# The first row group's adjacency of a graph attention kernel in eight transfers in place of sixteen

## The chip, the core and the metric

The kernel runs on one core of a Trainium2 chip. TensorE (PE) multiplies and transposes, VectorE (DVE), ScalarE (ACT) and GpSimd (POOL) do the rest, SyncE (SP) only issues transfers. Each engine works its own instructions in order and waits on semaphores. Transfers are issued by SP, ACT or POOL into a queue each and are carried out by 16 DMA engines that all queues share; a transfer is cut into packets, and its semaphore stands at 16 when all engines are done. The metric is the device time of one execution in microseconds (us): 810.08 us is the median of three runs (810.04 to 810.56).

## What is computed

One graph attention layer over 8192 nodes with 128 features, after a normalisation, with a residual:

```python
def _L0_gnn_ref(h, adj, W, a):
    Wh = h @ W                                   # 8192 x 128
    f1 = Wh @ a1 ; f2 = Wh @ a2                  # a score half for each node
    e = leaky_relu(f1[:, None] + f2[None, :], negative_slope=0.2)
    e = where(adj == 0, -inf, e)                 # adj: 8192 x 8192 int32, zeros and ones
    return softmax(e, axis=1) @ Wh
h = maximum(_layernorm(x, axis=-1), 0.0)
x = x + _L0_gnn_ref(h, adj, W, a)
```

The adjacency is 268 MB of int32. It is read once, and turned into bytes on the way, so that a value takes 4 bytes in DRAM and 1 byte in SBUF.

## The kernel before, in words

**Tiling.** The 8192 rows are 16 row groups of 512 (`NQ`); a partition holds four neighbouring rows of its group (`PACK`). The 8192 columns are 16 units of 512 (`UN`), four of which (`KC`) are a column group of 2048 (`CHUNK`). For each row group and each unit the kernel needs the adjacency of 512 by 512, transposes it, forms the weights and multiplies them into four accumulators.

**A unit's way.** ACT scales half of the unit's bytes (`second`, line 591), POOL adds the halves so that two edges share a byte (`mix`, line 239), PE transposes them (`transposes`, line 382), ACT unpacks the result into `marks` (`unpack`, line 571), DVE makes four tiles of weights (`weights`, line 811), and PE does 32 products with them (`product`, lines 392 and 396).

**The first row group** is worked while the features of all nodes are still being made, 4 tiles of nodes (a group `g` of 512 nodes) for each unit `b`. A loop of 16 steps `b` runs on all engines. In step `b` PE does the products of unit `b`, the features of group `b + 2` (line 365), and the transposes of the normalised x of group `b + 3` (line 349). ACT does `second(b + 3)`, keeps the features (`keep`, line 549), takes the exponentials (lines 561, 562), unpacks unit `b + 2`, applies the ReLU (line 542), and normalises a quarter of group `b + 4`. POOL does `mix(b + 2)`, `scaled(b + 2)` (line 267), three quarters of the normalisation of group `b + 4` (line 248), and issues transfers. DVE does the weights of unit `b + 1` with `low_part` (line 801), `pack(b + 2)` (lines 792, 793), and in the steps that the tables name the statistics of x (`statistics`, line 751) and the inverse roots of a batch (`inverses`, lines 768 to 773). All of this stands in an order written out by hand; in DVE's step 2 it is `first_weights(3)`, `inverses(3)`, `pack(4)`, `statistics(10)`, and in step 3 `first_weights(4)` comes next.

**Loading x.** x is 4 MB of float32 and comes in five batches of groups, `BATCHES = [(0, 1), (1, 4), (4, 6), (6, 10), (10, 16)]`, issued by SP (line 182). The first two are issued at once. Batches 2, 3 and 4 are held back by a wait on the adjacency of units 0, 1 and 3 (line 188). The first use of batch 3 is `statistics(6)` in DVE's step 0, the first use of batch 4 is `statistics(10)` in DVE's step 2.

**Loading the adjacency.** The first row group comes unit by unit: `load_part(u)` on POOL (line 224) moves, for 128 partitions and four rows of each, 512 values, 2 KB of DRAM into 512 bytes of SBUF, and has a semaphore of its own, `first_loaded[u]`. Units 0 to 9 are issued ahead of all other work of POOL (`EARLY`), units 10 and 11 ahead of the loop, 12 in step 0, 13 in step 1, 14 and 15 in step 2 (`PARTS`). All later row groups come in transfers of one row of a column group: 128 partitions of 2048 values each, 8 KB of DRAM into 2 KB of SBUF (`load`, line 214); the first of these are issued from step 3 on (`FIRSTS`, `HALVES`). POOL's and SP's transfers stand in two queues, q0 and q1 of the profile. POOL's is worked in the order of issue.

Of the kernel before, what the change touches and what calls it, by code (L numbers as in the profile page):

```python
# [38 lines left out]
P = 128  # L39
PACK = 4  # L40
BANK = 512
CHUNK = PACK * BANK
# [17 lines left out]
def gat_kernel(nc, x, adj, W, a, out):  # L60
# [5 lines left out]
    KC = CHUNK // BANK  # L66
    UN = NC * KC
# [3 lines left out]
    AHEAD = 6  # L71
    EARLY = 10
    HALF = PACK // 2
# [10 lines left out]
    MIXES = {13: (15, 16), 14: (17, 18), 15: (19,)}  # L84
    PARTS = {0: (12,), 1: (13,), 2: (14, 15)}
    FIRSTS = {3: 4, 6: 5, 10: 6, 14: 7}
# [6 lines left out]
    with ExitStack() as ctx:  # L93
# [6 lines left out]
        def sem(name):  # L100
# [4 lines left out]
        masks = sb("masks", [P, GC, CHUNK], U8)  # L105
# [31 lines left out]
            "adj_second0", "adj_second1", "adj_second2", "adj_second3",  # L137
            *(f"first_loaded{u}" for u in range(UN)),
            "ident_zero", "ident_ready", "cst_ready", "rows_done", "out_stored", "x_again",
# [8 lines left out]
        adj_second = [s[f"adj_second{c}"] for c in range(NC)]  # L148
        first_loaded = [s[f"first_loaded{k}"] for k in range(UN)]
        x_loaded = [s[f"x_loaded{k}"] for k in range(len(BATCHES))]  # L150
# [3 lines left out]
        adj_dram = adj.rearrange("(q p s) (c k) -> q s c p k", p=P, s=PACK, k=CHUNK)  # L154
        adj_first = adj.rearrange("(q p s) (b k) -> q b p s k", p=P, s=PACK, k=BANK)

# [55 lines left out]
        def _(pool):  # L212
# [8 lines left out]

            def load_part(u):
                c, k = u // KC, u % KC
                nc.gpsimd.dma_start(masks[:, c * PACK:(c + 1) * PACK, k * BANK:(k + 1) * BANK],  # L224
                                    adj_first[0, u]).then_inc(first_loaded[u], 16)

            for u in range(EARLY):
                load_part(u)
# [61 lines left out]
            mix(1)  # L290
            scaled(1)
            load_part(EARLY)
            load_part(EARLY + 1)
            for b in range(UN):
                for u in MIXES.get(b, (b + 2,)):
                    mix(u)
                if b + 2 < NQ:
                    scaled(b + 2)
                if b + 4 < NQ:
                    normalise(b + 4)  # L300
                for u in PARTS.get(b, ()):
                    load_part(u)
                if b in FIRSTS:
                    load_first(FIRSTS[b])
                if b in HALVES:
                    load_second(HALVES[b])
# [689 lines left out]
```

## Time and profile before

| | |
|---|---|
| median of three runs | 810.08 us (810.04 to 810.56) |
| profiled execution | 810.9 us, its span 809.2 us |
| PE busy | 785.9 us, 97% |
| DVE busy | 740.8 us, 92% |
| ACT busy | 483.5 us, 60% |
| POOL busy | 419.2 us, 52% |
| POOL's transfer queue (q0) | 67.13 MB written to SBUF, 87.8% of the DMA engines' time |
| DRAM read | 272.70 MB |

Times inside the span count from its start. The profiled execution took 1.7 us more than its span, and 0.8 us more than the median of the runs. Bytes and GB/s of a transfer are those that are written; a transfer of the adjacency reads four times as many. A packet is one run of values: four rows in each of 128 partitions make 512 packets for a unit, and 16 packets of 4 bytes raise the semaphore. The number of an issue that a landing belongs to is found by taking a narrow window of time around that issue.

### The profile page before, as it was taken

The page shows a single profiled execution, that of the slowest core. Times are in us where ns is not written, and L with a number is a line of the kernel's source. Part 1 is how long each engine was busy: PE and PEld are TensorE (multiplying, and loading weights), DVE is VectorE, ACT ScalarE, POOL GpSimd, SP SyncE. Part 2 cuts the span into 40 slices and gives each one's busy share as a digit, 9 for nine tenths or more (in the row PEclk, how much of TensorE's full clock was granted, in tenths as well). Part 3 has the DMA queues.
Part 4 walks back from the last instruction along what each step waited for, and adds up shares of the span by engine and source line. Part 5 has one row for each costly group of instructions (what it writes and reads, how often), then busy time and mean ns, then how long its engine had stood idle before and what let it go on. Part 6 is the DMA issues. An engine that isn't in the chain of part 4 may idle for free.

```text
span 809.2 us, 22590 instructions
## 1 busy us (share of the span) xinstructions
PE 785.9 (97%) x8969; PEld 718.5 (89%) x8969; DVE 740.8 (92%) x1189; ACT 483.5 (60%) x777; POOL 419.2 (52%) x621
## 2 busy tenths in 40 slices
PE   5899999999999999999999999999999999999997
PEld 4778799999999999999999999999999999999986
DVE  6997899999999999999999999999999999999996
ACT  6788865655655565565555556565555656555542
POOL 7687755544545554454545445454544545454320
PEclk9999999999999999999999999999999999999999
DMA  9998899999999999999999999999999999998200
GB/s 172 169 106 85 79 108 114 110 96 107 85 101 95 97 91 88 110 85 101 91 100 91 87 110 86 101 88 104 90 88 107 89 100 86 106 90 87 27 14 17
DMA packets 48321, 75.99 MB, mean 94 GB/s; under 512 B 4768, under 2 KB 13600, under 8 KB 48288
## 3 DMA queue, kind: packets, MB, share of 16 engines
q0 software_dynamic: 43008, 67.13, 87.8%
q1 hardware_dynamic: 4864, 8.39, 3.1%
q8 instruction: 17, 0.28, 0.1%
q14 instruction: 16, 0.13, 0.0%
q10 hardware_dynamic: 416, 0.07, 0.0%
HBM read 272.70 MB, written 4.19 MB: 342 GB/s over the span
## 4 chain that ended last, share of the span: by engine, by line
PE 90%; issue 3%; ACT 2%; DVE 2%; POOL 2%; DMA 1%; ACTq 0%; POOLq 0%; DVEq 0%
PE acc L392 53%; PE acc L396 27%; PE stage L382 7%; PE stage L365 2%; DVE wt_ring L811 1%; PE stage L373 1%; ACT ht L542 1%; DMA a_sb<-in_L_gnn_a_dram 1%; PE stage L349 1%; POOL xn L248 0%; ACT wh L549 0%; POOL tmp L267 0%; POOL masks L224 0%; POOL masks L239 0%; ACT tmp L562 0%
## 5 line engine op out<-in xcount | busy, mean ns | idle before, releaser
L811 DVE SCALAR_TENSOR_TENSOR wt_ring<-stage,packed,marks 128x512 f32<-128x512 f32 x1024 | 697.6, 743 | 54.1 <-PE acc L396 42.5
L392 PE MATMUL acc<-pairs,wt_ring 128*128 128x258 f16 x4096 | 718.9, 274 | 2.4 <-DVE pairs L801 1.3
L396 PE MATMUL acc<-pairs,wt_ring 128*128 128x129 f16 x4096 | 697.4, 219 | 0.0
L392 PEld LDWEIGHTS acc<-pairs,wt_ring 128*128 128x128 f16 x4096 | 396.0, 97 | 56.7 <-DVE pairs L801 2.2
L571 ACT ACTIVATE marks<-stage 128x1024 uint16<-128x1024 uint8 x256 | 262.0, 1023 | 290.5 <-PE stage L382 289.3
L396 PEld LDWEIGHTS acc<-pairs,wt_ring 128*128 128x128 f16 x4096 | 399.5, 98 | 2.5
L239 POOL TENSOR_TENSOR masks<-masks 128x256 int32<-128x256 int32 x256 | 184.2, 734 | 240.4 <-ACT masks L591 239.6
L214 POOL DMA_DIRECT2D masks<-in_adj_dram x240 | 130.3, 545 | 99.5 <-PE stage L382 77.5
L591 ACT ACTIVATE masks<-masks 128x512 uint16<-128x512 uint16 x256 | 158.9, 622 | 0.5 <-DMA masks<-in_adj_dram 0.5
L382 PE MATMUL stage<-ident,masks 128*128 128x128 f32 x512 | 99.2, 276 | 1.5 <-POOL masks L239 0.9
L382 PEld LDWEIGHTS stage<-ident,masks 128*128 128x128 f32 x512 | 53.0, 141 | 6.4 <-issue 2.8
L365 PE MATMUL stage<-wx,ht 128*128 128x130 f32 x124 | 22.2, 305 | 6.8 <-ACT ht L542 5.8
L365 PEld LDWEIGHTS stage<-wx,ht 128*128 128x128 f32 x124 | 17.7, 205 | 10.5 <-ACT ht L542 9.1
L267 POOL TENSOR_TENSOR tmp<-wh,tmp 128x512 f32<-128x512 f32 x16 | 17.9, 1120 | 16.5 <-ACT tmp L562 16.5
L274 POOL TENSOR_SCALAR fin<-fin 128x516 f32<-128x516 f32 x15 | 22.8, 1523 | 0.3
L608 ACT ACTIVATE fin<-acc 128x258 f32<-128x258 f32 x60 | 19.6, 388 | 3.2 <-PE acc L392 3.2
L248 POOL TENSOR_SCALAR xn<-xm,small 128x128 f32<-128x128 f32 x42 | 18.2, 441 | 1.9 <-DVE small L773 1.9
L614 ACT ACTIVATE fin<-fin,inv 128x128 f32<-128x128 f32 x60 | 19.0, 389 | 0.0
L549 ACT ACTIVATE wh<-stage 128x260 f32<-128x260 f32 x31 | 12.0, 387 | 10.8 <-PE stage L365 10.7
L284 POOL TENSOR_TENSOR xm<-fin,xm 128x512 f32<-128x512 f32 x15 | 18.0, 1203 | 0.1
L277 POOL TENSOR_TENSOR fin<-fin 128x516 f32<-128x516 f32 x15 | 16.5, 1102 | 1.3
L751 DVE BATCH_NORM_STATS2 stats<-xm 128x6 f32<-128x256 f32 x32 | 11.5, 415 | 3.1 <-DMA xm<-in_x_dram 3.1
(60 smaller groups left out, 143.9 us busy)
## 6 DMA issues: line engine op xcount, KB each, us to landing
masks<-in_adj_dram POOLq DMA_DIRECT2D x256, 256.0 KB, 7.4
out_dram<-xm SPq DMA_DIRECT2D x15, 256.0 KB, 7.2
xm<-in_x_dram SPq DMA_DIRECT2D x1, 1536.0 KB, 13.4
xm<-in_x_dram SPq DMA_DIRECT2D x1, 1024.0 KB, 10.5
xm<-in_x_dram SPq DMA_DIRECT2D x1, 768.0 KB, 5.8
xm<-in_x_dram SPq DMA_DIRECT2D x1, 512.0 KB, 7.6
xm<-in_x_dram SPq DMA_DIRECT2D x1, 256.0 KB, 3.2
out_dram<-xm SPq DMA_DIRECT2D x4, 64.0 KB, 2.6
```

What stands on the lines that cost most here:

```text
L214: nc.gpsimd.dma_start(masks[:, c * PACK + r, :], adj_dram[q, r, c]).then_inc(adj_loaded[c] if r < 2 else adj_second[c], 16)
L239: nc.gpsimd.tensor_tensor(edges4[:, c, 0, :, sl], edges4[:, c, 0, :, sl], edges4[:, c, 1, :, sl], ALU.add).then_inc(s["mixed"], 1)
L274: nc.gpsimd.tensor_scalar(fin[:, :, E1:2 * E1], fin[:, :, E1:2 * E1], 1.0 / LOW, None, ALU.mult).then_inc(s["lows_scaled"], 1)
L365: mm = nc.tensor.matmul(to[:, r * 256:r * 256 + WC], ht[:, g % 2, k:k + P], wx[:], start=(r == 0), stop=(r == 1), skip_group_check=True)
L382: mm = nc.tensor.transpose(stage[:, 0, r * P:(r + 1) * P], words[:, c * PACK + r, kk * P:(kk + 1) * P], ident[:])
L392: return nc.tensor.matmul(acc[:, r, 0:2 * E1], wtv[:, w, r, 1, :], pairv[:, t, :, 0:E1], start=st, stop=end)
L396: return nc.tensor.matmul(acc[:, r, 0:E1], wtv[:, w, r, 0, :], pairv[:, t, 0, 0:E1], start=False, stop=False)
L571: nc.scalar.activation(split[:, b % MR, :].rearrange("p (s w) -> p s w", s=PACK), stage[:, 0, 0:BANK // 2].bitcast(U8).rearrange("p (w s) ...
L591: nc.scalar.activation(twos[:, c, 1, :, sl], twos[:, c, 1, :, sl], ACT.Copy, scale=SECOND).then_inc(s["second_ready"], 1)
L608: nc.scalar.activation(fin[:, r, :], acc[:, r, 0:2 * E1], ACT.Copy).then_inc(s["acc_free"], 1)
L614: mm = nc.scalar.activation(fin[:, r, 0:Fo], fin[:, r, 0:Fo], ACT.Identity, scale=inv[:, r:r + 1])
L811: nc.vector.scalar_tensor_tensor(out=wtq[:, t % NW], in0=e_row, scalar=packed[:, t, 1:2], in1=edges[:, k], op0=ALU.max, op1=ALU.mult).then ...
```

## The change

The first row group's adjacency comes in eight transfers. `GROUPS` lists the units of each: four transfers of one unit, two of two units, two of four units, which is a whole column group. A transfer still has 128 partitions with four rows of each, so 512 packets whatever its width; a packet is now 2 KB, 4 KB or 8 KB of DRAM. Each transfer has one semaphore, and `first_loaded[u]` is the semaphore of the transfer that holds unit `u`. The first seven (units 0 to 11) are issued ahead of all other work of POOL, the eighth (units 12 to 15) ahead of the loop. The loop issues none of them, and the table `PARTS` is gone.

```diff
-    EARLY = 10
+    GROUPS = [(0, 1), (1, 2), (2, 3), (3, 4), (4, 6), (6, 8), (8, 12), (12, 16)]
+    EARLY = 7
...
-    PARTS = {0: (12,), 1: (13,), 2: (14, 15)}
...
-            *(f"first_loaded{u}" for u in range(UN)),
+            *(f"first_loaded{k}" for k in range(len(GROUPS))),
...
-        first_loaded = [s[f"first_loaded{k}"] for k in range(UN)]
+        first_loaded = [s[f"first_loaded{k}"] for k, (lo, hi) in enumerate(GROUPS) for u in range(lo, hi)]
...
-        adj_first = adj.rearrange("(q p s) (b k) -> q b p s k", p=P, s=PACK, k=BANK)
+        adj_first = adj.rearrange("(q p s) (c k) -> q c p s k", p=P, s=PACK, k=CHUNK)
...
-            def load_part(u):
-                c, k = u // KC, u % KC
-                nc.gpsimd.dma_start(masks[:, c * PACK:(c + 1) * PACK, k * BANK:(k + 1) * BANK],
-                                    adj_first[0, u]).then_inc(first_loaded[u], 16)
+            def load_part(n):
+                lo, hi = GROUPS[n]
+                c, k = lo // KC, lo % KC
+                sl = slice(k * BANK, (k + hi - lo) * BANK)
+                nc.gpsimd.dma_start(masks[:, c * PACK:(c + 1) * PACK, sl], adj_first[0, c, :, :, sl]
+                                    ).then_inc(first_loaded[lo], 16)
...
             load_part(EARLY)
-            load_part(EARLY + 1)
             for b in range(UN):
...
-                for u in PARTS.get(b, ()):
-                    load_part(u)
```

POOL's instructions from the first issue to step 1 of the loop, before (`masks` is the adjacency in SBUF, `tmp` the scaled features, `xn` the normalised x):

```order
L224 DMA masks<-in_adj_dram 128x4x512 x10
L239 TENSOR_TENSOR masks<-masks 128x2x128
L267 TENSOR_TENSOR tmp<-wh,tmp 128x4x128
L248 TENSOR_SCALAR xn<-xm,small 128x128 x6
L239 TENSOR_TENSOR masks<-masks 128x2x128
L267 TENSOR_TENSOR tmp<-wh,tmp 128x4x128
L224 DMA masks<-in_adj_dram 128x4x512 x2
L239 TENSOR_TENSOR masks<-masks 128x2x128
L267 TENSOR_TENSOR tmp<-wh,tmp 128x4x128
L248 TENSOR_SCALAR xn<-xm,small 128x128 x3
L224 DMA masks<-in_adj_dram 128x4x512
L239 TENSOR_TENSOR masks<-masks 128x2x128
```

The same stretch in the changed kernel (its line 227 is line 224 of before, 242 is 239, 270 is 267, 251 is 248):

```order
L227 DMA masks<-in_adj_dram 128x4x512 x4
L227 DMA masks<-in_adj_dram 128x4x1024 x2
L227 DMA masks<-in_adj_dram 128x4x2048
L242 TENSOR_TENSOR masks<-masks 128x2x128
L270 TENSOR_TENSOR tmp<-wh,tmp 128x4x128
L251 TENSOR_SCALAR xn<-xm,small 128x128 x6
L242 TENSOR_TENSOR masks<-masks 128x2x128
L270 TENSOR_TENSOR tmp<-wh,tmp 128x4x128
L227 DMA masks<-in_adj_dram 128x4x2048
L242 TENSOR_TENSOR masks<-masks 128x2x128
L270 TENSOR_TENSOR tmp<-wh,tmp 128x4x128
L251 TENSOR_SCALAR xn<-xm,small 128x128 x3
```

Ten issues have become seven, the two ahead of the loop have become one, and the one between the normalisation and the next `mix` is gone.

POOL's instructions from step 1 to step 3, before:

```order
L267 TENSOR_TENSOR tmp<-wh,tmp 128x4x128
L248 TENSOR_SCALAR xn<-xm,small 128x128 x3
L224 DMA masks<-in_adj_dram 128x4x512
L239 TENSOR_TENSOR masks<-masks 128x2x128
L267 TENSOR_TENSOR tmp<-wh,tmp 128x4x128
L248 TENSOR_SCALAR xn<-xm,small 128x128 x3
L224 DMA masks<-in_adj_dram 128x4x512 x2
L239 TENSOR_TENSOR masks<-masks 128x2x128
L267 TENSOR_TENSOR tmp<-wh,tmp 128x4x128
L248 TENSOR_SCALAR xn<-xm,small 128x128 x3
L214 DMA masks<-in_adj_dram 128x2048 x2
```

And in the changed kernel (its line 215 is line 214 of before):

```order
L270 TENSOR_TENSOR tmp<-wh,tmp 128x4x128
L251 TENSOR_SCALAR xn<-xm,small 128x128 x3
L242 TENSOR_TENSOR masks<-masks 128x2x128
L270 TENSOR_TENSOR tmp<-wh,tmp 128x4x128
L251 TENSOR_SCALAR xn<-xm,small 128x128 x3
L242 TENSOR_TENSOR masks<-masks 128x2x128
L270 TENSOR_TENSOR tmp<-wh,tmp 128x4x128
L251 TENSOR_SCALAR xn<-xm,small 128x128 x3
L215 DMA masks<-in_adj_dram 128x2048 x2
```

Three issues are gone from this stretch, and the transfers of the second row group come at the same place. The instructions of PE, DVE, ACT and SP stand as before.

## Rows read from the trace of the kernel before

**Rows 1.** Busy time by stretch: start:end, length, engines' busy us (instructions), clock, DMA, GB/s.

```profile
20.00:30.00 10.00, 8.14 (x68) 7.14 (x66) 9.83 (x23) 6.20 (x15) 5.32 (x8) 0.83 1.16 196
50.00:60.00 10.00, 9.26 (x96) 8.23 (x96) 9.76 (x23) 8.66 (x20) 7.21 (x13) 1.00 1.18 107
100.00:150.00 50.00, 50.00 (x587) 46.09 (x585) 46.39 (x71) 29.62 (x45) 26.42 (x41) 1.00 1.06 112
```

**Rows 2.** DVE's waits from 14 to 58 us, all: us in total, times, longest.

```profile
DVE wt_ring L811 <- PE stage L373: 1.3, 1, 1.3
DVE packed L792 <- ACT tmp L562: 0.4, 1, 0.4
```

**Rows 3.** DVE in order of time: start, us, engine, line, operation [idle before].

```profile
35.69 1.01 DVE L768 TENSOR_TENSOR small<-small 128x16 f32<-128x16 f32 x1
...
37.52 0.76 DVE L751 BATCH_NORM_STATS2 stats<-xm 128x6 f32<-128x256 f32 x2
38.20 2.71 DVE L811 SCALAR_TENSOR_TENSOR wt_ring<-stage,packed,marks 128x512 f32<-128x512 f32 x4
...
56.13 1.05 DVE L771 SCALAR_TENSOR_TENSOR small<-small 128x24 f32<-128x24 f32 x1
...
62.37 2.73 DVE L811 SCALAR_TENSOR_TENSOR wt_ring<-stage,packed,marks 128x512 f32<-128x512 f32 x4 [0.87 <-ACT marks L571]
```

**Rows 4.** The transfer of x's last batch, issued at 21.3 us.

```profile
L182 SPq DMA_DIRECT2D xm<-in_x_dram x1: 380/380/380, 21.3 to 21.3; - x1
...
DMA to landing us min/median/max: 13.4/13.4/13.4
```

**Rows 5.** Packets of each queue from 25 to 32 us: packets, MB, share.

```profile
q1 hardware_dynamic: 655, 1.34, 56.5%
q0 software_dynamic: 655, 0.33, 54.9%
```

**Rows 6.** The same from 140 to 142.5 us, a store beside the adjacency.

```profile
q0 software_dynamic: 105, 0.20, 79.8%
q1 hardware_dynamic: 104, 0.21, 24.9%
```

**Rows 7.** The same from 0 to 24.9 us.

```profile
q0 software_dynamic: 2928, 1.46, 70.2%
```

**Rows 8.** The same from 45 to 50 us, adjacency alone.

```profile
q0 software_dynamic: 1027, 0.51, 122.7%
```

**Rows 9.** The same from 61 to 66 us, adjacency alone.

```profile
q0 software_dynamic: 293, 0.53, 106.5%
```

**Rows 10.** Line 224's issues of units 4 and 5.

```profile
L224 POOL DMA_DIRECT2D masks<-in_adj_dram x2: 742/742/742, 5.0 to 5.8; - x2
...
DMA to landing us min/median/max: 19.1/21.3/23.5
```

**Rows 11.** Line 224's issues of units 6 and 7.

```profile
L224 POOL DMA_DIRECT2D masks<-in_adj_dram x2: 740/740/740, 6.5 to 7.2; - x2
...
DMA to landing us min/median/max: 28.0/28.9/29.8
```

**Rows 12.** ACT in order of time.

```profile
26.94 0.62 ACT L591 ACTIVATE masks<-masks 128x512 uint16<-128x512 uint16 x1
29.60 0.39 ACT L549 ACTIVATE wh<-stage 128x260 f32<-128x260 f32 x1 [2.04 <-PE stage L365]
...
38.72 0.62 ACT L591 ACTIVATE masks<-masks 128x512 uint16<-128x512 uint16 x1
```

**Rows 13.** POOL in order of time.

```profile
35.36 1.31 POOL L267 TENSOR_TENSOR tmp<-wh,tmp 128x512 f32<-128x512 f32 x1 [0.89 <-ACT tmp L562]
...
38.69 1.55 POOL L224 DMA_DIRECT2D masks<-in_adj_dram  x2
...
56.10 1.05 POOL L267 TENSOR_TENSOR tmp<-wh,tmp 128x512 f32<-128x512 f32 x1 [1.83 <-ACT tmp L562]
```

**Rows 14.** PE in order of time.

```profile
41.14 0.41 PE L382 MATMUL stage<-ident,masks 128*128 128x128 f32 x2 [0.51 <-POOL masks L239]
```

**Rows 15.** Busy time in two short stretches, columns as in rows 1.

```profile
26.00:29.30 3.30, 3.30 (x20) 2.98 (x19) 3.30 (x7) 1.18 (x3) 2.13 (x4) 0.50 1.12 241
...
36.50:37.70 1.20, 0.17 (x2) 0.01 (x1) 1.06 (x7) 0.61 (x2) 0.44 (x2) 1.00 1.26 105
```

## The prediction

> **What bounds the kernel now.** I read the busy time by stretch first. From 100 us on PE is busy for the whole stretch, 50.00 of 50.00 us, and DVE for 46.39 [rows 1]; fifteen of the sixteen row groups run there at PE's pace, and nothing in the change touches them. What the change can move is when that part begins, which is decided in the first 100 us. There no engine is full except one: DVE is busy for 9.83 of 10 us from 20 us on, and for 9.76 from 50 us on, with PE at 8.14 and 9.26 [rows 1]. So I asked for DVE's waits. From 14 to 58 us there are two, 1.3 us at the first weights and 0.4 us for an exponential [rows 2]. From 31 us on DVE has no wait. It works without a pause until step 7 of the loop; then it waits 0.87 us for ACT at 62.37 us [rows 3], and ACT and PE set the pace of the later steps. From 31 to about 58 us a saving on another engine therefore buys nothing, and each microsecond for which DVE has to wait goes into the end time.
>
> **Next, the transfers.** The DMA share is above 1 in all three stretches [rows 1], so they queue. From 25 to 32 us the adjacency (q0) and the last batch of x (q1) run beside each other and move 655 packets each [rows 5]. One takes turns with the other, packet by packet. On this the prediction rests.
>
> **What is removed on POOL.** Eight issues at 0.74 us [rows 10, 11], 5.9 us of POOL's time. Three of them are ahead of all work and one ahead of the loop, where POOL waits for ACT next. The last two, 1.55 us at 38.69 us [rows 13], do delay something: PE waits 0.51 us for the `mix` behind them [rows 14]. PE and ACT could be about half a microsecond earlier there. But DVE has no wait in this stretch [rows 2], so what arrives earlier for it stays lying. Value: 0. Bounds: if DVE were not the engine that decides, 0.5 us gained; on the other side 0.1 us lost, should the wider transfers cost more to issue (the number of packets that POOL writes for each is the same).
>
> **What the adjacency's own widths cost.** A unit of a wide transfer can be used only when all of it has landed.
> - Units 4 and 5. Unit 4 landed at 24.1 us (5.0 + 19.1) and unit 5 at 29.3 us (5.8 + 23.5) [rows 10]; ACT takes unit 4 at 26.94 us [rows 12]. It now comes with unit 5. Below I get 26.6 us for the last packet and about 28.4 us for the landing. ACT's piece of 0.62 us then ends at 29.0 us, and the next one on ACT starts at 29.60 us, after 2.04 us of idle time [rows 12]. The wait is hidden. If the pair landed as late as unit 5 did, ACT's next would start 0.3 us late.
> - Units 6 and 7. The second landed at 37.0 us (7.2 + 29.8) [rows 11], ACT takes the first at 38.72 us [rows 12]. Hidden. Units 8 to 15 have at least as much room.
>
> **What they cost x.** The last batch of x is 768 packets of 2 KB, 48 for each DMA engine. It is issued at 21.3 us and lands 13.4 us later, at 34.7 us [rows 4]. DVE takes it at 37.52 us, with 2.8 us to spare [rows 3]. While it shares the engines a pair of packets, one of each queue, takes 7 us / (655/16) = 0.171 us [rows 5]. 48 pairs are 8.2 us; the other 5.2 us are the way to the first packet and the engines that finish late, and I keep them.
>
> In the changed kernel the packet on the other side of each pair is wider. With 8 KB of adjacency beside 2 KB of x a pair takes 2.5 us / (104.5/16) = 0.383 us, from a store beside the later transfers, again one to one [rows 6]. No row has 4 KB; it lies a third of the way from 2 to 8 KB, and so I take 0.171 + 0.212/3 = 0.242 us. That also fits the packets alone: 5 us / (1027/16) = 0.078 us for 2 KB and 5 us / (293/16) = 0.273 us for 8 KB, semaphore packets counted in [rows 8, 9]. The ends for 4 KB are those two rows, 0.171 and 0.383 us; the value is the one nearer to its bytes.
>
> Which packets stand beside x? At 24.9 us, when sharing begins, 2928 packets of the adjacency have gone, five units of 528 and 288 of the sixth [rows 7]. So about three quarters of the bytes of units 4 and 5 are through, and some 7 of the pair's 32 packets for each engine are left. Then come 32 packets of units 6 and 7, also of 4 KB. That is 39 of x's 48. The other 9 run beside the 8 KB packets of units 8 to 11.
>
> T = 39 x 0.242 + 9 x 0.383 = 9.4 + 3.4 = 12.9 us instead of 8.2 us. The batch lands 4.7 us later, at 39.4 us, and the 2.8 us to spare are gone. DVE, ready at 37.5 us, stands still for 1.9 us in front of `statistics(10)`. Behind it in DVE's queue are the weights of unit 4, which start at 38.20 us [rows 3], the pairs and everything else of steps 3 to 7. PE waits for these. (7 x 0.242 us behind 24.9 us is the 26.6 us used above, and 1.8 us from last packet to landing is what unit 5 had: last packet near 27.5 us, half its packets being left at 24.9 us, landing at 29.3 us.)
>
> **What lies behind the stall.** Twice DVE's small operations of `inverses` take about 1.0 us instead of 0.17 while POOL works on line 267: 35.69 us against 35.36, and 56.13 against 56.10 [rows 3, 13]. The first meeting is ahead of the stall. At the second POOL has moved too, by less than DVE, since PE and ACT have some room; at best 0.1 us is saved. The PE wait of 0.51 us [rows 14] vanishes, as DVE is later than that anyway.
>
> **Weighed against a rule.** The two rows with packets of 2 KB and of 8 KB beside 2 KB both show one for one [rows 5, 6]. The Trainium skill, in "DMA: Bandwidth & Descriptors", section "Queues, rings and completion order", has an engine drain a whole packet of several descriptors from one queue before it turns to the other, and in "SWDGE vs HWDGE vs iDMA" such a packet is preferably at most 4096 bytes. By that rule two 2 KB pieces of x would go for each 8 KB piece of the adjacency. By that rule two pieces of x beside one of 4 KB are as many bytes as two pairs of rows 5, so T would stay at about 8.2 us, and the sum would be that of rival 1, 810.0 us, instead of 811.9. The rows so far speak against the rule.
>
> **The sum.** 1.9 - 0.1 = +1.8 us. Against the profiled execution 810.9 + 1.8 = 812.7 us (its span 811.0); it stands 0.8 us above the median of the runs, so the median becomes 811.9 us.
>
> **The rivals.**
> 1. *Shares by bytes.* If a turn is a number of bytes rather than one piece, x keeps its half of the bandwidth, the batch lands near 34.7 us, and nothing waits. Then only the contention and POOL's issues are left: 0 to 0.3 us less, 810.0 us. For it: x loaded beside 4 KB pieces is in no row, and rows 6 are a store. Against it: one for one in both rows, at a ratio of 1 and of 4. 20%.
> 2. *The stall and the low clock.* PE ran at 0.50 of its clock from 26.0 to 29.3 us [rows 15], in the middle of the loop. 0.50 is 1.2 of 2.4 GHz. If the new pause near 42 us brings such a stretch again, PE's 3.3 us of work there would have been about 1.65 us at the full clock, and with half of the difference or all of it on the path the time is 1.9 + 0.8 to 1.7 us, 812.7 to 813.6 us. Also in this case: x's late engines being late in proportion (5.2 us becomes 6). Against it: from 36.5 to 37.7 us PE was busy for only 0.17 us, and its clock stayed at 1.00 [rows 15]. 15%.
> 3. *The freed POOL counts.* If the 0.5 us of PE [rows 14] and the 0.4 us of DVE [rows 2] both come back and x is in time after all: 810.1 - 0.9 = 809.2 us. This decides if the batch lands before 37.5 us, which needs T under 11 us, a pair of 4 KB under 0.19 us. 12%.
> 4. *The change does not do what it says*, the wide transfers being cut into the same 2 KB packets: then the ring holds what it held, and the time is that of before, 810.0 us. 3%.
>
> **How the numbers follow.** The forecast has 50%. Its own range goes by the ends of the pair: at 0.21 us for 4 KB, T is 11.6 us, the batch lands at 38.1 us and the time is 810.6 us; at 0.27 us, T is 13.9 us, it lands at 40.4 us and the time is 812.9 us. The far ends, 0.171 and 0.383 us, give T of 10.1 and 18.4 us, no stall and one of 7.4 us, 810.0 and 817.4 us; the upper one would need a 4 KB packet to take as long as one of 8 KB, and I leave it out. The predicted time is 811.9 us. The range that should hold 8 in 10 reaches down into rivals 1 and 4 and up into rival 2: 809.7 to 813.3 us. This kernel's measurement tells about 0.2% from no change, 1.6 us: below 808.5 us is faster, above 811.7 us slower. Nothing that I can name reaches 808.5 us; I leave 7% for what I have not seen and for rival 3. Slower holds most of the forecast, the upper part of it, and rival 2: 48%. The same: 45%.
>
> **What would show it.** In the profile of the changed kernel: DVE's `statistics(10)` (line 751) with a wait of 1 to 3 us for the transfer of x near 37.5 us; x's last batch landing 17 to 19 us after its issue; as many packets of q1 as of q0 from 25 to 32 us, some 460 each; ACT waiting about 1.4 us for unit 4 near 27 us, with the next piece at 29.6 us as before; PE without its wait at 41.14 us, but with one for DVE near 42 us; and the first interval in which PE is full starting 1.8 us later, with the same pace after it. Wrong: no wait of DVE for x, or a stretch after 100 us that runs at another pace.

## The result, and the profile after

The changed kernel takes 813.55 us (median of six runs, 813.24 to 814.45), the kernel before 810.58 us beside it (six runs, 810.04 to 810.79). The ratio is 1.0041, with a 95% interval of 1.0029 to 1.0053 (it is estimated from the single runs; the quotient of the two medians is 1.0037): slower, by 3.0 us between the medians. The forecast was 811.9 us, 1.8 us slower. The profiled execution took 813.58 us, its span 811.8 us.

The chain ahead of the loss came as forecast. Both rows of x's last batch, and DVE's waits from 14 to 62 us, all of them, in the changed kernel (against [rows 4] and [rows 2]; its line 183 is line 182 of before):

```profile
L183 SPq DMA_DIRECT2D xm<-in_x_dram x1: 381/381/381, 21.2 to 21.2; - x1
...
DMA to landing us min/median/max: 17.8/17.8/17.8
```

```profile
DVE stats L751 <- DMA xm<-in_x_dram: 1.6, 1, 1.6
DVE wt_ring L811 <- PE stage L373: 1.3, 1, 1.3
```

The batch lands 17.8 us after its issue instead of 13.4, at 39.0 us, and DVE waits 1.6 us for it. Packets of each queue from 25 to 32 us, with pieces of 4 KB of adjacency, and from 35 to 37.5 us, with pieces of 8 KB (against [rows 5, 6]):

```profile
q0 software_dynamic: 464, 0.46, 68.9%
q1 hardware_dynamic: 459, 0.94, 39.5%
```

```profile
q0 software_dynamic: 110, 0.21, 83.2%
q1 hardware_dynamic: 103, 0.20, 23.5%
```

Again one packet for one. A pair with 4 KB takes 7 / (461.5/16) = 0.243 us (0.242 had been worked out), one with 8 KB 2.5 / (106.5/16) = 0.376 us (0.383). Units 4 and 5 hold ACT for 1.46 us, where it waited for PE before [rows 12]; ACT in order of time:

```profile
28.53 0.63 ACT L591 ACTIVATE masks<-masks 128x512 uint16<-128x512 uint16 x1 [1.46 <-DMA masks<-in_adj_dram]
29.07 0.37 ACT L549 ACTIVATE wh<-stage 128x260 f32<-128x260 f32 x1
```

What had not been forecast stands behind the stall. DVE in order of time (against [rows 3]), then POOL (its line 270 is 267 of before, its 251 is 248):

```profile
38.99 0.76 DVE L751 BATCH_NORM_STATS2 stats<-xm 128x6 f32<-128x256 f32 x2 [1.63 <-DMA xm<-in_x_dram]
39.67 2.71 DVE L811 SCALAR_TENSOR_TENSOR wt_ring<-stage,packed,marks 128x512 f32<-128x512 f32 x4
...
47.14 1.44 DVE L801 SCALAR_TENSOR_TENSOR pairs<-pairs,tmp 128x516 f16<-128x516 f16 x1
...
52.74 1.43 DVE L801 SCALAR_TENSOR_TENSOR pairs<-pairs,tmp 128x516 f16<-128x516 f16 x1
...
60.53 2.73 DVE L811 SCALAR_TENSOR_TENSOR wt_ring<-stage,packed,marks 128x512 f32<-128x512 f32 x4
...
65.18 1.41 DVE L811 SCALAR_TENSOR_TENSOR wt_ring<-stage,packed,marks 128x512 f32<-128x512 f32 x2 [0.87 <-ACT marks L571]
```

```profile
46.97 1.05 POOL L270 TENSOR_TENSOR tmp<-wh,tmp 128x512 f32<-128x512 f32 x1 [1.47 <-ACT tmp L562]
48.01 1.75 POOL L251 TENSOR_SCALAR xn<-xm,small 128x128 f32<-128x128 f32 x3
...
52.57 1.05 POOL L270 TENSOR_TENSOR tmp<-wh,tmp 128x512 f32<-128x512 f32 x1 [0.96 <-ACT tmp L562]
```

The weights of unit 4 start 1.47 us later than before (39.67 against 38.20). Those of unit 8 start 2.81 us later, 60.53 us against 57.72 us, and the same 2.81 us stand at the next wait for ACT (65.18 against 62.37). So 1.34 us are lost between them, with no wait in the list. They are in the duration of two pair operations (line 801), 1.44 and 1.43 us where those of steps 3 and 6 take 0.69 and 0.68: each starts 0.17 us after POOL's product and ends 0.6 us after the product has ended. In the kernel before, DVE's pair operation came first in both steps; its DVE, then its POOL:

```profile
45.72 0.68 DVE L801 SCALAR_TENSOR_TENSOR pairs<-pairs,tmp 128x516 f16<-128x516 f16 x1
...
50.66 0.68 DVE L801 SCALAR_TENSOR_TENSOR pairs<-pairs,tmp 128x516 f16<-128x516 f16 x1
...
57.72 2.73 DVE L811 SCALAR_TENSOR_TENSOR wt_ring<-stage,packed,marks 128x512 f32<-128x512 f32 x4
```

```profile
46.45 1.05 POOL L267 TENSOR_TENSOR tmp<-wh,tmp 128x512 f32<-128x512 f32 x1 [0.83 <-ACT tmp L562]
...
51.23 1.05 POOL L267 TENSOR_TENSOR tmp<-wh,tmp 128x512 f32<-128x512 f32 x1 [0.59 <-ACT tmp L562]
```

Behind 100 us the weights of the units start at 104.21, 107.12 and 110.02 us, where before they started at 101.38, 104.28 and 107.19: later by 2.83 us, at the same pace.

One relation holds over all the traces of this document. From the start of unit 9's weights (62.37 us before, 65.18 us here) to the time of that execution it is 748.5 and 748.4 us, and in each of the eighteen traces of the experiments 748.2 to 748.6 us. So whatever the variants change has happened by then, and that start can be read in place of the time.

### The profile page after: what moved, and what is told of

Read it like the earlier page. It is cut to its first block, busy times and chain, and to the rows that moved or that the text cites. A ratio compares the mean times of both kernels' runs of the same rounds, so it can differ in the third digit from the quotient of the medians.

```text
span 811.8 us, 22582 instructions
## 1 busy us (share of the span) xinstructions
PE 784.7 (97%) x8969; PEld 717.6 (88%) x8969; DVE 742.6 (91%) x1189; ACT 483.9 (60%) x777; POOL 415.7 (51%) x613
## 4 chain that ended last, share of the span: by engine, by line
PE 88%; DMA 4%; DVE 4%; issue 1%; ACT 1%; POOL 0%; ACTq 0%; DVEq 0%; POOLq 0%
PE acc L392 52%; PE acc L396 27%; PE stage L382 7%; DVE wt_ring L811 2%; DMA xm<-in_x_dram 2%; DMA masks<-in_adj_dram 2%; PE stage L365 1%; PE stage L373 1%; ACT ht L542 1%; DVE pairs L801 0%; DVE stats L751 0%; PE stage L349 0%; POOL masks L227 0%; ACT wh L549 0%; ACT tmp L562 0%
## 6 DMA issues: line engine op xcount, KB each, us to landing
xm<-in_x_dram SPq DMA_DIRECT2D x1, 1536.0 KB, 17.8
```

## The experiments

All ran beside the kernel before; times are medians in us, that of the kernel before from the same chip. The ratio is estimated from the single runs and is not the quotient of the medians. Where a variant leaves out work, the quoted expectation says which. Lines of kernel.py move by a few where a variant adds some; the names are the same.

| run | what differs | time | before | ratio, 95% interval |
|---|---|---|---|---|
| e1 | units 4 to 7 single again | 810.12 | 810.39 | 0.9999 [0.9990, 1.0008] |
| e2 | statistics one step later | 810.29 | 810.39 | 1.0001 [0.9992, 1.0010] |
| e3 | changed kernel, products of groups 6, 7 cut | 812.99 | 810.39 | 1.0036 [1.0022, 1.0050] |
| e4 | the same in the kernel before | 810.33 | 810.39 | 1.0000 [0.9991, 1.0009] |
| e5 | only units 4 to 7 in pairs | 812.28 | 810.39 | 1.0016 [1.0006, 1.0025] |
| e6 | kernel before, x held back | 814.49 | 810.39 | 1.0047 [1.0034, 1.0061] |
| e7 | changed kernel, products of groups 4 to 9 cut | 812.05 | 810.39 | 1.0019 [1.0010, 1.0028] |
| e8 | the same in the kernel before | 809.49 | 810.39 | 0.9988 [0.9979, 0.9997] |
| e9 | x's last batch earlier | 811.10 | 810.56 | 1.0008 [0.9998, 1.0017] |
| e10 | inverses later, step 2 | 811.53 | 810.56 | 1.0009 [1.0000, 1.0018] |
| e11 | inverses later, steps 0 and 2 | 810.72 | 810.56 | 1.0003 [0.9994, 1.0012] |
| e12 | e1 and e11 together | 809.82 | 810.56 | 0.9992 [0.9983, 1.0001] |
| e13 | e5, products of groups 5 to 7 cut | 810.45 | 810.53 | 1.0001 [0.9992, 1.0010] |
| e14, e15 | e5 again, one traced execution each | 812.44, 810.30 | 810.53 | |
| e16 | changed kernel, products of groups 5 to 7 cut | 813.07 | 810.53 | 1.0035 [1.0022, 1.0049] |
| e17, e18 | e16 again, one traced execution each | 812.88, 813.00 | 810.60 | |

### Does the loss come through x? e1, e2, e9, e6

The theory was that the transfers cost only by making x's last batch late, and the rival that their width, the late unit 4 or the number of issues cost in themselves.

e1, narrow packets while x is under way:

```diff
-    GROUPS = [(0, 1), (1, 2), (2, 3), (3, 4), (4, 6), (6, 8), (8, 12), (12, 16)]
-    EARLY = 7
+    GROUPS = [(0, 1), (1, 2), (2, 3), (3, 4), (4, 5), (5, 6), (6, 7), (7, 8), (8, 12), (12, 16)]
+    EARLY = 9
```

> The changed kernel with units 4 to 7 in transfers of one unit again; units 8 to 11 and 12 to 15 stay in one transfer each (nine issues ahead of all work, the tenth ahead of the loop). Theory (x's last batch is late because it takes turns with wider packets): the batch again runs beside 2 KB packets only and lands near 34.7 us, DVE has no wait for it near 37 us, no collision follows, and the time is within 0.5 us of the kernel before (810.3 to 811.0 when that measures 810.6). Rival (it is the wide transfers of units 8 to 15 or the number of issues as such): a good part of the 3.0 us stays, 812 us or more.

810.12 us. The batch lands 13.3 us after its issue, and there is no wait for it.

e2, the wide transfers with x asked for later:

```diff
-    STATS = {0: (6, 7), 1: (8, 9), 2: (10,), 3: (11, 12), 4: (13, 14), 5: (15,)}
+    STATS = {0: (6, 7), 1: (8, 9), 3: (10, 11), 4: (12, 13), 5: (14, 15)}
```

> The changed kernel with all its transfers as they are; only the statistics of x's group 10 move on DVE from step 2 to step 3, and one group each from step 3 to 4 and from 4 to 5. Theory: the batch still lands near 39 us, but DVE asks for it only behind the weights of unit 4, near 41 us, and does not wait; the loss of 3.0 us goes but for collisions with POOL, which the shifted order can put elsewhere: 810.3 to 811.9 us. Rival (the transfers cost through something else, a late unit or slower engines): 813 us or more, with or without a wait of DVE.

810.29 us. The batch lands 17.6 us after its issue, as late as in the changed kernel, DVE does not wait, and the pair operations of steps 3 to 5 take 0.69 us. With every transfer of the change in place the loss is gone: the rival has fallen. The shifted order alone, in the kernel before, was not run; that it did not by itself win back 3 us rests on e1, which keeps the order and comes to the same time.

e9, the wide transfers with x issued earlier:

```diff
-            for k, part in ((2, 0), (3, 1), (4, 3)):
+            for k, part in ((2, 0), (3, 1), (4, 2)):
```

> The changed kernel, all transfers as they are, but x's last batch is issued when unit 2 has landed (16 us) instead of unit 3 (21.2 us). Theory (the loss hangs on the landing of that batch): it starts behind batch 3 at about 22 us, runs beside 4 KB packets only (48 pairs at 0.243 us, 11.7 us), and lands between 34.5 and 36 us, so DVE has no wait at 37 us; but the pair of units 4 and 5 now shares all its time and lands near 29.7 us instead of 28.5, which holds ACT 1 us longer, with 0.5 us of room: 810.2 to 811.9 us when the kernel before measures 810.4. Rival (the transfers cost otherwise): 813 us.

811.10 us, in the range expected. The batch is issued at 15.6 us and lands 19.0 us later, at 34.6 us. ACT now waits 2.2 us for units 4 and 5. DVE has no wait for x, and no pair operation of steps 3 to 5 is long. The 0.5 us that are left are not clear of noise, as the interval holds 1.

e6, the kernel before with x alone made late:

```diff
-            for k, part in ((2, 0), (3, 1), (4, 3)):
+            for k, part in ((2, 0), (3, 1), (4, 5)):
```

> The kernel before with all its transfers, but x's last batch is issued when unit 5 has landed (29.3 us) instead of unit 3 (21.3 us). Theory (what costs is the time at which that batch lands, whatever makes it late): it lands near 42.5 us, DVE waits 4.5 to 5.5 us for it, and as DVE has no room up to step 7, the time rises by that wait and by up to 1.5 us of collisions with POOL: 815 to 817.3 us. Rival (DVE's chain has slack behind the wait, and it was the collisions that cost): less than 4 us, below 814.4 us.

814.49 us, 4.1 us slower. That is between the expected range (815 and more) and the rival's (below 814.4): the batch is issued at 28.3 us and lands at 40.7 us, earlier than I had worked out, and the collisions with POOL did not come. DVE's wait and the weights of units 4, 5 and 6 behind it:

```profile
40.76 0.76 DVE L751 BATCH_NORM_STATS2 stats<-xm 128x6 f32<-128x256 f32 x2 [3.25 <-DMA xm<-in_x_dram]
41.44 2.71 DVE L811 SCALAR_TENSOR_TENSOR wt_ring<-stage,packed,marks 128x512 f32<-128x512 f32 x4
...
46.28 2.71 DVE L811 SCALAR_TENSOR_TENSOR wt_ring<-stage,packed,marks 128x512 f32<-128x512 f32 x4
...
51.98 2.71 DVE L811 SCALAR_TENSOR_TENSOR wt_ring<-stage,packed,marks 128x512 f32<-128x512 f32 x4
```

The weights of unit 4 start 3.24 us later than before, those of unit 5 3.18 (before at 43.10), those of unit 6 3.95 (before at 48.03). The wait comes out whole, and 0.8 us are added in step 4. No pair operation is long behind the wait; PE's clock is low in this stretch, from 45 to 48 us (below), and DVE waits 0.76 us for an exponential of ACT at 50.35 us. With no wide transfer and no meeting behind it, the wait for x alone costs its whole length.

### The second half: DVE behind POOL. e3, e4, e7, e8

```diff
-                nc.gpsimd.tensor_tensor(tmp[:, g % 2, :, 0:Fo], wh[:, g * PACK:(g + 1) * PACK, 0:Fo],
-                                        tmp[:, g % 2, :, Fo:E1].to_broadcast([P, PACK, Fo]), ALU.mult
+                n = 8 if g in (6, 7) else Fo
+                nc.gpsimd.tensor_tensor(tmp[:, g % 2, :, 0:n], wh[:, g * PACK:(g + 1) * PACK, 0:n],
+                                        tmp[:, g % 2, :, Fo:E1].to_broadcast([P, PACK, n]), ALU.mult
```

e3 is this in the changed kernel, e4 in the kernel before; e7 and e8 are the same pair with `4 <= g < 10`, e16 the changed kernel with `g in (5, 6, 7)`.

> The changed kernel, in which POOL's product for the scaled features of groups 6 and 7 handles 8 of 128 columns (the rest of those two tiles is left out). Theory (half of the loss is DVE's pair operation, line 801 of before, standing behind that product twice, 0.75 us each): both pair operations take 0.69 us again instead of 1.44, the wait for x stays at 1.6 us, and the time falls by 1.2 to 1.6 us, to about 812.1 us. Rival (the long pair operations are in parallel to something that decides, all the loss is the wait for x): 813.3 to 813.7 us.

> The kernel before with the same cut as in e3 (POOL's product for groups 6 and 7 handles 8 of 128 columns), as the control. There the pair operations took 0.68 us and met nothing. Theory: no change, 810.3 to 810.9 us. Rival (the shorter POOL work gains in itself): 1 us or more less, below 809.6 us.

e4 changed nothing, as expected. In e3's profile (812.2 us) both pair operations take 0.69 us again, the wait for x is 1.5 us, and the weights of unit 9 start at 63.69 us instead of 65.18: 1.49 us earlier:

```profile
63.69 2.73 DVE L812 SCALAR_TENSOR_TENSOR wt_ring<-stage,packed,marks 128x512 f32<-128x512 f32 x4 [0.87 <-ACT marks L572]
```

But the five runs lie from 811.78 to 814.07 us, and their median is only 0.6 us under that of the changed kernel. The trace agreed with the theory and the runs did not yet.

> The changed kernel, in which POOL's product for the scaled features of groups 4 to 9 handles 8 of 128 columns (the rest of six tiles is left out), so that DVE's small-tile operations cannot stand behind it. Theory (loss = wait for x, 1.5 us, plus collisions, 1.4 us): against the same cut in the kernel before (e8) it is 1.3 to 1.8 us slower, not 3.0. Rival (all of the 3.0 us follows from the wait, the long operations stood in its shadow): 3 us slower than e8.

> The kernel before with the same cut as in e7. Before, two operations of the inverses stood 0.85 us each behind that product while DVE had no room. Theory: both fall to 0.17 us and the time by 0.8 to 1.7 us, to 808.7 to 809.6 us. Rival (DVE's time is not what decides there): 810.2 to 810.6 us.

e8 is 0.9 us faster, at the small end of the 0.8 to 1.7 us expected: both operations of the inverses take 0.17 us in its trace, and the weights of unit 9 start at 61.25 us, 1.12 us earlier. Of the 1.7 us that the two meetings seem to cost, about two thirds come out. e7 missed. It is 2.6 us slower than e8, not 1.3 to 1.8. Its profile shows why: without the meeting of step 2 DVE comes to the statistics earlier, at 36.3 us, while x lands at 39.4 us, so the wait is 3.2 us instead of 1.6, and the weights of unit 4 start at 40.13 us against 37.66 us in e8, 2.47 us later. A saving ahead of the stall is lost in it. The comparison does not tell the meetings apart, as it changed the wait too.

### Two kinds of runs of one program. e5, e13, e14, e15

e5 has pairs for units 4 to 7 and single units from 8 on:

```diff
-    GROUPS = [(0, 1), (1, 2), (2, 3), (3, 4), (4, 6), (6, 8), (8, 12), (12, 16)]
-    EARLY = 7
+    GROUPS = [(0, 1), (1, 2), (2, 3), (3, 4), (4, 6), (6, 8)] + [(u, u + 1) for u in range(8, 16)]
+    EARLY = 8
+    PARTS = {0: (10,), 1: (11,), 2: (12, 13)}
...
             load_part(EARLY)
+            load_part(EARLY + 1)
...
+                for u in PARTS.get(b, ()):
+                    load_part(u)
```

> The kernel before with only units 4 and 5 and units 6 and 7 in one transfer each; units 8 to 15 stay single, as before (eight issues ahead of all work, two ahead of the loop, then one, one and two in steps 0, 1, 2). Theory (one packet of x for one packet of adjacency): 39 pairs at 0.243 us and 9 at 0.171 us are 11.0 us, so x's last batch lands 16.2 us after its issue, at 37.1 to 37.5 us, as DVE comes to it: a wait of 0 to 0.4 us, and 810.2 to 811.2 us when the kernel before measures 810.4. Rival (the late unit 4 or the wider pieces cost in themselves, not through x): 812 us or more. Rival (x is late only through the 8 KB packets): it lands below 36 us.

x's last batch lands 16.0 us after its issue, at 37.0 us, 0.2 us sooner than worked out. The time was not as expected, and the median of 812.28 us is what the rival had named (that the late unit 4 or the wider pieces cost in themselves). But the median hides two kinds: of eleven runs four are at 810.3 to 810.6 us and seven at 812.0 to 813.1. So the program was run twice more for its trace, and once with the products of groups 5, 6 and 7 cut.

> e5 with POOL's product for groups 5, 6 and 7 on 8 of 128 columns (the rest of those three tiles is left out). e5's eleven runs fall into two kinds, four at 810.3 to 810.6 us and seven at 812.0 to 813.1 us; its one profile, of the slower kind, has DVE's pair operation at 1.07, 1.44 and 1.43 us instead of 0.69, each time beside that product. Theory (the two kinds are the runs without and with these meetings): with the product cut all runs are of the quicker kind, 810.2 to 811.2 us. Rival (the kinds come from when x lands, or from the clock): the runs keep two kinds 2 us apart.

> e5 once more, for its trace. Theory: if its time is near 810.4 us, the pair operations of steps 3 to 5 take 0.69 us; if near 812.5 us, two or three of them take over 1.0 us. Rival: the long ones are there at either time.

> As e14: e5 once more for its trace. Theory: the time follows the number of long pair operations, 0.75 us each. Rival: it does not.

e13: all eleven runs from 810.25 to 811.04 us. The second kind has gone, with unit 4 as late and the pieces as wide as in e5, so that rival has fallen too. e14 and e15 happened to be one of each kind. DVE's pair operations from 40.3 to 54 us in the groups of e14 (812.44 us), then of e15 (810.30 us): line, names, shapes, count, busy us, mean ns:

```profile
L805 DVE SCALAR_TENSOR_TENSOR pairs<-pairs,tmp 128x516 f16<-128x516 f16 x3 | 4.3, 1421 | 0.0
```

```profile
L805 DVE SCALAR_TENSOR_TENSOR pairs<-pairs,tmp 128x516 f16<-128x516 f16 x3 | 2.1, 685 | 0.0
```

Three operations (line 805 here is 801 of before), 2.2 us between them, and 2.1 us between the times. Their starts beside POOL's product in step 4, e14 first, then e15:

```profile
46.18 1.43 DVE L805 SCALAR_TENSOR_TENSOR pairs<-pairs,tmp 128x516 f16<-128x516 f16 x1
```

```profile
46.01 1.05 POOL L271 TENSOR_TENSOR tmp<-wh,tmp 128x512 f32<-128x512 f32 x1 [0.96 <-ACT tmp L566]
```

```profile
45.41 0.68 DVE L805 SCALAR_TENSOR_TENSOR pairs<-pairs,tmp 128x516 f16<-128x516 f16 x1
```

```profile
46.02 1.05 POOL L271 TENSOR_TENSOR tmp<-wh,tmp 128x512 f32<-128x512 f32 x1 [0.70 <-ACT tmp L566]
```

POOL starts at the same time in both. DVE is ahead of it in e15 and just behind it in e14, and then waits until it ends. In step 3 the two start closest, DVE and POOL of e14, then DVE and POOL of e15:

```profile
40.62 1.40 DVE L805 SCALAR_TENSOR_TENSOR pairs<-pairs,tmp 128x516 f16<-128x516 f16 x1
```

```profile
40.42 1.05 POOL L271 TENSOR_TENSOR tmp<-wh,tmp 128x512 f32<-128x512 f32 x1
```

```profile
40.57 0.68 DVE L805 SCALAR_TENSOR_TENSOR pairs<-pairs,tmp 128x516 f16<-128x516 f16 x1
```

```profile
40.55 1.61 POOL L271 TENSOR_TENSOR tmp<-wh,tmp 128x512 f32<-128x512 f32 x1
```

In e14 POOL is let through and DVE's operation is the long one, in e15 it is the other way round. Once DVE has lost one meeting it is late for the next. That these meetings make up the two microseconds is shown by e13, which takes them away, and not only by the order of the rows. What tips an execution to one kind or the other is not shown. From e15 to e14 DVE's start in step 3 moves by 0.05 us and POOL's by 0.13 us the other way; e14 had waited 0.3 us for x and e15 had no such wait in the list, but that wait accounts for the 0.05 us at most.

The Trainium skill states this in "SBUF — State Buffer", section "SBUF: two separate sides": an exclusive lock on a pair of ports, for the whole instruction, between a DVE operation with two inputs in SBUF and a POOL operation that reads SBUF, and whoever starts first has it. The traces agree in both directions, with DVE held in e14 (1.40 us) and POOL in e15 (1.61 us); the starts of e15's step 3, with POOL's put 0.02 us ahead, are too close to tell which came first.

### The other runs: PE's clock. e16, e17, e18

> The changed kernel with the product of groups 5, 6 and 7 on 8 of 128 columns (e3 cut 6 and 7 alone, and its five runs lay from 811.8 to 814.1 us). Theory (wait for x 1.5 us plus meetings 1.4 us): the meetings of steps 3 to 5 are gone in all runs, 811.6 to 812.4 us, 1.2 to 1.9 us slower than the kernel before. Rival (something else than the meetings makes up the second half of the loss): runs at 813 us and more, as in e3.

The profile (812.16 us) was as the theory says, all pair operations of steps 3 to 5 at 0.69 us; the other four runs were at 812.5 to 814.5 us, which the rival had expected. Two more traced executions of the same program:

> e16 once more, for its trace (groups 5, 6 and 7 of POOL's product on 8 of 128 columns). Theory: at 813 us and more there is a stretch of PE's low clock (3.4 us at 0.50) behind the wait for x, as in the profiles of e6 and e7 from 44.9 us on; near 812.2 us there is none. Rival: the slower runs have long pair operations or a longer wait for x.

> As e17: e16 once more for its trace. Theory: the time follows the low clock behind the wait for x. Rival: it follows the wait itself or DVE's operations.

e17 took 812.88 us and e18 813.00 us. Both had the pair operations of steps 4 and 5 at 0.69 us, e18's of step 3 at 0.94, and in both PE's clock was low behind the stall. Busy time from 45.2 to 48 us, of e16, then of e17, columns as in rows 1:

```profile
45.20:48.00 2.80, 2.43 (x27) 2.07 (x26) 2.77 (x7) 2.11 (x6) 1.08 (x2) 1.00 1.08 115
```

```profile
45.20:48.00 2.80, 2.80 (x20) 2.62 (x18) 2.75 (x5) 0.80 (x3) 0.00 (x0) 0.60 1.06 111
```

The second of ACT's two keeps of group 6 in the same stretch, of e16, then of e17:

```profile
45.93 0.39 ACT L550 ACTIVATE wh<-stage 128x260 f32<-128x260 f32 x1 [0.66 <-PE stage L366]
```

```profile
47.75 0.39 ACT L550 ACTIVATE wh<-stage 128x260 f32<-128x260 f32 x1 [2.00 <-PE stage L366]
```

PE's features come 1.8 us later, DVE then waits 0.7 us for an exponential, and the weights of unit 9 stand at 64.55 us in e17 and 64.44 in e18, against 63.63 in e16: 0.8 to 0.9 us. The times differ by 0.7 and 0.8. The low clock was there in e6 and e7 too, each behind a wait of over 3 us, not in the profile of the changed kernel. The kernel before and e3 had such a stretch near 26 us, e17 a first one near 20 us, all ahead of the stall.

For the runs without a trace there is one more number, the mean granted clock of each. Of e16's five, the two at 0.999 took 812.16 (the traced one) and 812.54 us, the three at 0.996 and 0.997 took 813.07 to 814.45 us. Of the changed kernel's six, the two at 0.999 took 813.58 (traced) and 813.41 us. So where the clock was undisturbed in both, the cut of the products is worth 0.9 to 1.4 us, near the 1.34 us of the trace, though these are two runs of each. Among the others it does not come out: the four runs of the changed kernel at 0.994 to 0.996 took 813.24 to 814.45 us. The clock does not order all runs either (one of e3 took 814.07 us at 0.998). What brings the low stretch in one execution and not in another stays open.

### Taking the meetings away by order. e10, e11, e12

```diff
-                if b in ROOTS:
+                if b in ROOTS and b not in (2,):
                     inverses(ROOTS[b])
...
                 for g in STATS.get(b, ()):
                     statistics(g)
+                    if b in (2,) and g == STATS[b][0]:
+                        inverses(ROOTS[b])
```

e11 has `(0, 2)` in place of `(2,)`, e12 is e1 with e11's order.

> The kernel before, in whose DVE step 2 the inverse roots stand behind the packing and the statistics of group 10 instead of ahead of them, so that they no longer meet POOL's product (35.4 to 36.4 us in the kernel before, 1.0 us instead of 0.17 for one operation). Theory (DVE decides from 31 to 58 us, so 0.85 us of collision taken away comes out in the end): 809.4 to 810.0 us when the kernel before measures 810.4. Rival (the gain is lost at a later collision or on PE's side): 810.2 us or more.

811.53 us, no gain, where up to 1 us was expected: 1.0 us slower by the medians, with an interval that begins at 1.0000. DVE's weights of unit 4 start 0.3 us earlier than before, but those of unit 5 0.4 us later: the inverses end later, and behind them on POOL stand the normalisation, two issues and only then the `mix` on which PE, ACT and the weights of unit 5 wait. Another 0.4 us are added in step 4, where DVE waits for an exponential, and the weights of unit 9 start 0.83 us later than before. POOL in e10:

```profile
38.06 1.31 POOL L248 TENSOR_SCALAR xn<-xm,small 128x128 f32<-128x128 f32 x3 [2.31 <-DVE small L773]
39.33 1.56 POOL L224 DMA_DIRECT2D masks<-in_adj_dram  x2
40.90 0.90 POOL L239 TENSOR_TENSOR masks<-masks 128x256 int32<-128x256 int32 x1
```

> The kernel before with that order in DVE's steps 0 and 2 (in both the packing and the statistics of one group come first). Theory: also the first collision, at 23.6 us, goes, up to 0.85 us more, if the normalisation of group 4, which comes 0.4 us later for POOL, does not take it back: 808.6 to 809.8 us. Rival: x's last batch (34.7 us) is now late for DVE, or a collision arises elsewhere: no better than e10, or 810.4 us and more.

810.72 us, no better than before. In step 0 nothing is gained: the meeting only moves to another small operation (a copy, line 831, takes 1.02 us at 23.64 us), and the weights of unit 2 start at 26.86 us where they started at 26.82. Those of unit 4 start 1.34 us earlier, from steps 1 and 2; 1.1 us of it are spent in steps 3 and 4 as in e10, and 0.2 us are left at unit 9 (62.17 us).

> e1 (units 0 to 7 single, then two transfers of four units) with the order of e11. Theory: e1's transfers cost and gain nothing by themselves, so the time is that of e11 within 0.4 us. Rival (with DVE faster, POOL's freed issue slots count): 0.5 us or more below e11.

809.82 us, 0.9 us under e11, as the rival expected. In steps 0 to 2 of the loop it has no issues, and its `mix` stands right behind the normalisation:

```profile
36.62 1.32 POOL L251 TENSOR_SCALAR xn<-xm,small 128x128 f32<-128x128 f32 x3 [0.85 <-DVE small L773]
37.90 0.73 POOL L242 TENSOR_TENSOR masks<-masks 128x256 int32<-128x256 int32 x1
```

Its weights of unit 5 start 5.26 us behind those of unit 4, in e11 it is 5.62 us. So the freed issues are worth something as soon as DVE's order is another. With the order of before they are worth nothing (e1). Whether e12 beats the kernel before can't be told: the interval is 0.9983 to 1.0001.

## Why the prediction was wrong, point by point

**Which engine decides: right.** DVE's wait comes out in the end, in the changed kernel (1.47 us at the weights of unit 4) and in e6 (3.24), and so does each later shift, since the time follows the start of unit 9's weights in every trace.

**POOL's issues worth 0: right** (e1: 810.12 against 810.39 us, interval 0.9990 to 1.0008), for as long as DVE has the order of before; e12 shows where that ends.

**Units 4 and 5 hidden: right for DVE, but not by the hole that was named.** Landing at 28.5 us for 28.4, and no wait of DVE behind it. ACT's idle 2.04 us [rows 12] belonged to the execution with PE's clock at 0.50 [rows 15]. At the full clock, in e1, ACT waits 0.66 us there and goes on at 27.96 us; in the changed kernel it goes on at 29.07 us, 1.1 us later, and not at 29.6 us as before. DVE did not feel it (unit 3's weights at 32.18 us, in e1 at 32.37). That the delay stayed off the path was luck as far as the argument goes.

**x's delay: right.** 0.243 us for 0.242, 0.376 for 0.383, landing at 39.0 us for 39.4, a wait of 1.6 us for 1.9. 464 packets stood beside 459. The turns are of one packet each: cut into 28 stretches of 0.25 us, 25 to 32 us has 15 to 18 packets of q0 and 15 to 19 of q1 in every one, about one of each for each of the 16 engines. The prediction had set aside the rule of the Trainium skill in "DMA: Bandwidth & Descriptors", section "Queues, rings and completion order", by which an engine drains a packet of several descriptors before it turns (a packet there is more than one piece, a packet of the profile is one). The trace of the changed kernel does not agree with it either: turns of several packets would leave one queue further ahead in some of these stretches. Equal counts over 7 us would not have told that by themselves; they only speak against turns by bytes.

**What lies behind the stall: wrong, and this is the step that failed.** The prediction had looked at DVE's meetings with POOL, priced one at 0.85 us, and then followed only the one that was already there, with "at best 0.1 us is saved" (0.03 us were: 1.02 us at 58.54 us for 1.05). The shift itself makes new ones. DVE was moved by the wait against POOL, whose product had started behind DVE's pair operation in step 4 and too late to hold it in step 5, and both pair operations now fall behind it: 1.34 us where -0.1 had been put. The sum with the measured terms is 1.47 + 1.34 = 2.8 us; the two profiled executions are 2.7 us apart, the medians 3.0 us. That the meetings cost their length is shown by taking them away: cleanly for e5 (e13), for the changed kernel in the traces of e3 and e16 (1.5 us at unit 9's weights). Its median falls by only 0.6 and 0.5 us with the cut. In e17 and e18 the low clock takes back 0.8 to 0.9 us; that it does so in the untraced runs near 814 us too is not shown. In the prediction's range such a meeting had no term, and the top at 813.3 us missed the 813.55 us.

**The rival with the low clock** had 15% and put 0.8 to 1.7 us on the path, up to 813.6 us, where the changed kernel came out. In the changed kernel's profile no such stretch was there, so it is not what made that execution slow. In e17 and e18, in which no meeting of steps 3 to 5 was left, it came with 0.8 to 0.9 us. So the stretch and its price are real, but it is not the cause of the time that was profiled here, and a hit of this rival's number would have been luck.

**The signs the prediction named:** the wait for x, the landing, the equal packets, ACT's wait and the vanished wait of PE at 41 us are all in the trace; PE waits 1.77 us for DVE at 43.04 us. The rise of the start of the full stretch was to be 1.8 us and is 2.8.

## What to carry to other kernels

A wider transfer took a larger share from the queue beside it, since the turns here were by packet, at 2, 4 and 8 KB: find the transfer with the least room that runs beside it and work out its landing by packets, not by bytes. Where an engine has no wait left, a stall costs its own length and then what the shift does to every pair of operations of two engines that hold each other up; list the gaps in which the other's operations stand, and ask which of them the shift closes. A program in which two such operations start within a tenth or two of a microsecond of each other can have two times, as e5 has, and one profile shows only one of them.

## What the runs showed of the hardware that was not expected

- One program with two times, 2.1 us apart in two traces without a stretch of low clock. The traces part at 40.6 us, where two engines start within 0.2 us of each other (e14, e15); with the other engine's operation cut, all runs are of one kind (e13).
- The holding goes both ways. The product of POOL holds DVE's pair operation for up to 0.75 us, and the pair operation holds the POOL operation that it overlaps: the three pieces of a normalisation took 1.75 us together (48.01 and 53.61 us in the changed kernel) instead of 1.31, and 1.78 us in e3 (47.24 us), where the product is cut and the pair operation takes 0.68.
- A stretch of about 3.4 us at half of PE's clock came in some executions and not in others of one program: near 44 us in e17 and e18, where it cost 0.8 to 0.9 us, and not in e16. In the kernel before it stood near 26 us in one trace, and e1 and e2, without it, started unit 9's weights 0.6 to 0.7 us earlier; how much of that is the clock is not shown.
